# Front of a hybrid attention kernel by batch, with gate keys over all 102 rows

## The reference

```python
x = x + attn_a(layernorm(x), W)
x = x + ffn(layernorm(x), gate_w, expert_bias, w1, w2, w3)
x = x + attn_b(layernorm(x), ...)
x = x + ffn(layernorm(x), ...)

def attn_a(x, W):                    # B, T, C = 4, 512, 128; 16 heads of 8
    q, k, v, gate = split(x @ W.T)   # 128, 128, 128, 16 columns
    log_G = cumsum(log_sigmoid(gate), axis=time)
    S = Q @ K.T                      # a head
    Z = 2*log(abs(S) + 1e-7) + log(scale) + log_G[t] - log_G[s]
    Z = where(s <= t, Z, -inf)
    P = exp(Z - rowmax(Z))
    return (P @ V) / sum(P)
```

## Time and profile before

| | before |
|---|---|
| median of the timed runs | 573.21 us |
| span of the profiled execution | 602.3 us |
| PE busy | 470.7 us (78%) |
| DVE busy | 334.1 us (55%) |
| ACT busy | 334.9 us (56%) |
| POOL busy | 305.8 us (51%) |
| mean granted TensorE clock | 0.857 |

### The profile page before, as it was taken

How to read it: one execution, slowest core, us unless ns; L and a number is a source line. 1 busy time by engine, 2 the same in 40 slices (tenths; PEclk the granted TensorE clock), 3 DMA queues, 4 the chain that set the end, 5 groups by cost and what they waited for, 6 DMA issues and landing times. The chain is left out here.

```text
span 602.3 us, 11488 instructions
## 1 busy us (share of the span) xinstructions
PE 470.7 (78%) x3813; PEld 332.8 (55%) x3813; DVE 334.1 (55%) x786; ACT 334.9 (56%) x656; POOL 305.8 (51%) x323
## 2 busy tenths in 40 slices
PE   2745998889989688789885897994789876779891
PEld 1333575556556455457564575773457664457670
DVE  4747884875885898232561276746366737032121
ACT  1553895876796766635652355465356445334350
POOL 3102573564473326837637475743565842566651
PEclk9985695977798676899998799998799988798896
DMA  5065064153165910201311311112311112241213
GB/s 143 6 142 99 7 156 83 42 120 69 23 151 174 196 74 10 56 23 43 73 65 47 95 41 40 29 35 87 110 35 32 38 30 87 59 125 42 47 37 118
DMA packets 36563, 43.52 MB, mean 72 GB/s; under 512 B 5996, under 2 KB 31492, under 8 KB 36484
## 3 DMA queue, kind: packets, MB, share of 16 engines
q1 hardware_dynamic: 30620, 30.72, 20.1%
q0 software_dynamic: 5888, 12.07, 8.1%
HBM read 25.91 MB, written 15.86 MB: 69 GB/s over the span
## 5 line engine op out<-in xcount | busy, mean ns | idle before, releaser
L1295 POOL DMA_INDIRECT token_out<-ysb,id_out x92 | 93.6, 1017 | 112.0 <-ACT ysb L1454 88.1
L933 POOL TENSOR_TENSOR PP<-PP,E 128x512 f32<-128x512 f32 x64 | 82.3, 1287 | 96.3 <-ACT PP L884 96.1
L1514 DVE TENSOR_TENSOR hid<-silu,ps 128x352 f32<-128x352 f32 x92 | 47.8, 520 | 147.1 <-PE ps L1376 87.9
L837 DVE TENSOR_SCALAR A<-ps 128x1024 int32<-128x1024 int32 x80 | 96.7, 1221 | 29.0 <-PE ps L742 26.5
L1287 POOL DMA_INDIRECT tiled<-scaled_rows,id_in x92 | 91.5, 995 | 26.7 <-issue 24.0
L884 ACT ACTIVATE PP<-A,feps 128x1024 f32<-128x1024 f32 x80 | 91.9, 1149 | 15.9 <-DVE A L837 15.8
L1355 ACT ACTIVATE turned<-ps 128x512 f32<-128x512 f32 (+2 forms) x104 | 56.9, 547 | 73.1 <-PE ps L1343 49.7
L1389 PE MATMUL ps<-room,turned 128*128 x552 | 82.0, 287 | 18.1 <-ACT ysb L1454 15.6
L1373 PE MATMUL ps<-room,turned 128*128 x184 | 78.7, 511 | 17.8 <-ACT silu L1447 14.0
L1389 PEld LDWEIGHTS ps<-room,turned 128*128 128x128 f32 x552 | 72.5, 200 | 21.7 <-issue 21.6
L1376 PE MATMUL ps<-room,turned 128*128 x184 | 75.6, 495 | 0.0
(11 more groups left out here) (211 smaller groups left out, 651.7 us busy)
## 6 DMA issues: line engine op xcount, KB each, us to landing
QS<-parts SPq DMA_DIRECT2D x24, 192.0 KB
KS<-parts SPq DMA_DIRECT2D x24, 192.0 KB
parts<-room SPq DMA_DIRECT2D x32, 128.0 KB, 2.4
scaled_rows<-xT SPq DMA_DIRECT2D x8, 512.0 KB
yb<-token_out SPq DMA_DIRECT2D x8, 512.0 KB, 4.0
room<-in_L_ffn_w_dram SPq DMA_DIRECT2D x2, 1408.0 KB, 9.2
tiled<-scaled_rows,id_in POOLq DMA_INDIRECT x92
token_out<-ysb,id_out POOLq DMA_INDIRECT x92
```

The source lines that it names most:

```text
L837: v.tensor_scalar(A[:, U % 3, :].bitcast(I32), ps[:, bank:bank + 2, :].rearrange("p k t -> p (k t)").bitcast(I32), 0x7fffffff, None, ALU.b ...
L933: g.tensor_tensor(w, w, E[:, hh % 4, :], MUL).then_inc(s_PD, 1)
L1295: g.indirect_dma_start(yr_d[m], bass.IndirectOffsetOnAxis(ap=id_out[:, m % 2, s:s + 1], axis=0), ysb[:, J % OUTS, :], None).then_inc(s_ret ...
L1514: v.tensor_tensor(hid[:, J % 2, 0:HID], silu[:, J % 2, :], ps[:, BK_B + J % 2, 0:HID], MUL).then_inc(s_hid, 1)
```

## The change

- Norms go by batch, each batch waits for its own part of x; the weights are loaded behind the first batch's x.
- K is projected ahead of Q. The gates' inputs are copied ahead of the values.
- The gates go in two units, batch 0 and batches 1 to 3; the bounds in three, 0, 1, and 2 with 3. The maximum over partitions is a turn on TensorE, a maximum of the row on DVE, a diagonal of it, and a product with ones, in place of POOL's reduction.
- Batch 0 and 1's parts are made by DVE alone in the front. The first stack is read for four heads first, K's rows ahead of Q's.
- The totals, parts, rows and differences of the second gate unit, the last bound and the clears stand in slots 0 to 8 (`FRONT`). Up to slot 9 the differences use one bank.
- The keys of the gates hold 102 rows, zeros in 0 to 95, set by POOL once; the products of the differences run over all 102 rows of QS.

```diff
-        def gate_keys(G, r):
-            own, n = slice(96, 102), T // 2
-            free = xh[own, (2 + G % 2) * TB:(3 + G % 2) * TB, :].rearrange("p i c -> p (i c)")
...
-            return (free[:, 0:n], free[:, n:2 * n], *other)[r].bitcast(BF16)
+        def gate_keys(G, r, own=slice(0, 102)):
+            n = T // 2
+            if G % 2 == 0:
+                return tiled[own, 4 * C + n * r:4 * C + n * r + n].bitcast(BF16)
+            free = xh[own, 3 * TB:4 * TB, :].rearrange("p i c -> p (i c)")
+            return (free[:, 0:n], free[:, n:2 * n], WT[own, 0:n], keys[own, :])[r].bitcast(BF16)
+
+        def key_rows_pool(odd):
+
+            g = nc.gpsimd
+            if not odd:
+                g.wait_ge(s_std, B)
+                link(g.memset(tiled[0:96, 4 * C:12 * C], 0.0), who="pool")
+                g.memset(tiled[96:99, 4 * C:12 * C].bitcast(BF16), 1.0).then_inc(s_ones, 1)
+                g.wait_ge(s_ones, 1)
+                return
+            g.wait_ge(s_const, NCONST)
+            g.wait_ge(s_vzp, B)
+            for r in range(GH):
+                link(g.memset(gate_keys(1, r, slice(0, 96)).bitcast(F32), 0.0), who="pool")
+                ones3 = g.memset(gate_keys(1, r, slice(96, 99)), 1.0)
+                if r < GH - 1:
+                    link(ones3, who="pool")
+            ones3.then_inc(s_ones, 1)
+            g.wait_ge(s_ones, 2)
...
+        GATE_UNITS = ((0,), (1, 2, 3))
+        BOUND_UNITS = ((0,), (1,), (2, 3))
+        BK_M = 7
...
             for b in range(B):
-                sp.dma_start(xt[:, TB * b:TB * b + TB, :], x_rows[:, TB * b:TB * b + TB, :]).then_inc(s_x, 16)
-            sp.dma_start(Wrows[:, :, :], W[0:3 * C, :].rearrange("(n p) c -> p n c", p=P)).then_inc(s_w, 16)
-            sp.dma_start(Wgr[:, :], W[3 * C:3 * C + H, :]).then_inc(s_w, 16)
-            sp.dma_start(gwr[:, :], gate_w).then_inc(s_w, 16)
+                sp.dma_start(xt[:, TB * b:TB * b + TB, :], x_rows[:, TB * b:TB * b + TB, :]).then_inc(s_x[b], 16)
+                if b == 0:
+                    sp.dma_start(Wrows[:, :, :], W[0:3 * C, :].rearrange("(n p) c -> p n c", p=P)).then_inc(s_w, 16)
+                    sp.dma_start(Wgr[:, :], W[3 * C:3 * C + H, :]).then_inc(s_w, 16)
+                    sp.dma_start(gwr[:, :], gate_w).then_inc(s_w, 16)
...
             sp, b = nc.sync, G // NG
             if G < 2:
-                sp.wait_ge(s_vzp, 3 + G)
-                for r in range(GH):
-                    gates = gate_keys(G, r)[0:3].rearrange("p (n c) -> p n c", c=P)
-                    sp.dma_start(gates, bc(onesb[0:3, :].unsqueeze(1), [3, gates.shape[1], P])).then_inc(s_keys[G], 16)
+                sp.wait_ge(s_ones, G + 1)
             else:
                 sp.wait_ge(s_D, GH * (G - 1))
             for r in range(GH):
-                sp.dma_start(gate_keys(G, r)[3:6], gates_d[b, 1, :, GH * (G % NG) + r, :]).then_inc(s_keys[G % 2], 16)
+                sp.dma_start(gate_keys(G, r, slice(99, 102)), gates_d[b, 1, :, GH * (G % NG) + r, :]).then_inc(s_keys[G % 2], 16)
...
+        def first_stack_sync():
+
+            sp = nc.sync
+            sp.wait_ge(s_part, 4)
+            store_sync(0, 1)
+            sp.wait_ge(s_store, 16 * 5)
+            rows_of_sync(0, 0, 1, 0, GH, s_early)
+            sp.wait_ge(s_part, PARTS)
+            store_sync(0, 0)
+            sp.wait_ge(s_store, STORES)
+            rows_of_sync(0, 0, 0, 0, GH, s_early)
+            gates_sync(0)
+            sp.dma_start(QS[96:99, 0, 0:8, :], gates_d[0, 0, :, 0:8, :]).then_inc(s_early, 16)
+            keys_sync(0)
+            rows_of_sync(0, 0, 1, GH, GH, s_stack[0])
+            rows_of_sync(0, 0, 0, GH, GH, s_stack[0])
+            keys_sync(1)
...
+            rows_of_sync(b, slot, 0, 8 * half, 8, s_stack[slot])
+            rows_of_sync(b, slot, 1, 8 * half, 8, s_stack[slot])
...
-            norm_root_half(1)
-            bound_pool(0)
+            for b in range(1, B):
+                norm_root(0, b)
+            key_rows_pool(False)
...
-            bound_pool(1)
+            key_rows_pool(True)
...
+        def bound_turn_tensor(u):
+            pe = nc.tensor
+            bs = BOUND_UNITS[u]
+            n = 2 * len(bs)
+            pe.wait_ge(s_mx, 2 * (bs[-1] + 1))
+            if u == 0:
+                pe.wait_ge(s_wTc, 2)
+            pe.transpose(ps[0:n, BK_M, 0:P], mx[:, bs[0]:bs[-1] + 1, :].rearrange("p b n -> p (b n)"), ident[:, :]).then_inc(s_mxt, 1)
+
+        def bound_spread_tensor(u):
+            pe = nc.tensor
+            n = 2 * len(BOUND_UNITS[u])
+            pe.wait_ge(s_most, u + 1)
+            pe.matmul(ps[:, BK_M, P:P + n], ones[0:n, :], mostd[0:n, u, 0:n], start=True, stop=True).then_inc(s_mxa, 1)
...
+        def gate_sums_tensor(u):
 
             pe = nc.tensor
-            pe.wait_ge(s_lg, hf + 1)
+            pe.wait_ge(s_lg, u + 1)
             pe.wait_ge(s_const, 5)
-            if hf:
+            if u:
                 pe.wait_ge(s_gt, 1)
-            for o, m in ((0, tri), (HT * H, ones)):
-                ins = pe.matmul(ps[:, 6, o:o + HT * H], m[:, :], lg[:, HT * hf:HT * hf + HT, :].rearrange("p t h -> p (t h)"),
+            t, n = unit_tiles(u), TB * H * len(GATE_UNITS[u])
+            for o, m in ((0, tri), (n, ones)):
+                ins = pe.matmul(ps[:, 6, o:o + n], m[:, :], lg[:, t, :].rearrange("p t h -> p (t h)"), start=True, stop=True)
+            ins.then_inc(s_gp, 1)
...
+            src = ps[:, 4:6, :].rearrange("p k (n c) -> p (k n) c", n=2)
+            a.activation(z[:, batch(b), :], src[:, :, C:C + H], ACT.Copy).then_inc(s_z, 1)
...
+            for k in range(2):
+                i = TB * b + 2 * k
+                src = ps[:, 4 + k, :].rearrange("p (n c) -> p n c", n=2)[:, :, 0:C]
+                ins = a.activation(va[:, i:i + 2, :, 0:HS], src.rearrange("p n (h d) -> p n h d", h=H), ACT.Copy)
+            ins.then_inc(s_vz, 1)
+
...
         AT_NORMAL = (8, 9, 10)
+        FRONT = {'totals': 0, 'parts': 1, 'rows': {2: 1, 3: 2, 4: 3}, 'differences': 5, 'clear': {1: 5, 3: 6},
+                 'bounds': {5: 2, 6: 3}, 'most': 7, 'scale': 8}
+        T_STARTS = 10
...
-                other = len(diff_banks) % 2 and U not in X_TAKEN and U < X_ENDS
+                other = len(diff_banks) % 2 and U not in X_TAKEN and T_STARTS <= U < X_ENDS
...
-            if p == 0 and half == 0:
-                pe.wait_ge(s_stack[slot], STACKS * (b + 1))
+            if p == 0 and G == 0:
+                pe.wait_ge(s_early, 16 * 7)
+            elif p == 0 and (half == 0 or G == 1):
+                pe.wait_ge(s_stack[slot], stacked(n))
             if p == 0:
-                pe.wait_ge(s_keys[G % 2], 16 * GH * (G // 2 + 2))
+                if G < 2:
+                    pe.wait_ge(s_ones, G + 1)
+                pe.wait_ge(s_keys[G % 2], 16 * GH * (G // 2 + 1))
...
-                    pe.matmul(dst[:, P * j:P * j + P], gate_keys(G, r)[:, P * j:P * j + P], QS[96:102, slot, h, P * j:P * j + P],
+                    pe.matmul(dst[:, P * j:P * j + P], gate_keys(G, r)[:, P * j:P * j + P], QS[:, slot, h, P * j:P * j + P],
...
+                if U == FRONT['totals']:
+                    gate_sums_tensor(1)
+                if U in FRONT['rows']:
+                    gate_turn_tensor(FRONT['rows'][U])
+                if U == FRONT['most']:
+                    bound_turn_tensor(2)
+                if U == FRONT['scale']:
+                    bound_spread_tensor(2)
...
-            v.wait_ge(s_vz, 2 * B)
-            for k in (BK_OFF, BK_DIA):
-                v.memset(ps[:, k, :], 0.0).then_inc(s_zb, 1)
...
-                if b + 1 < B and k in (0, 3, 4, 7, 8):
+                if U == FRONT['totals']:
+                    gate_totals_vector(1)
+                if U == FRONT['parts']:
+                    gate_parts_vector(1)
+                if U in FRONT['rows']:
+                    gate_rows_vector(FRONT['rows'][U])
+                if U == FRONT['differences']:
+                    gate_differences_vector(1)
+                if U in FRONT['bounds']:
+                    for n in range(2):
+                        bound_vector(FRONT['bounds'][U], n)
+                if U == FRONT['most']:
+                    bound_most_vector(2)
+                if U == FRONT['scale']:
+                    bound_scale_vector(2)
+                if U in FRONT['clear']:
+                    if U == 1:
+                        v.wait_ge(s_vz, B)
+                    v.memset(ps[:, FRONT['clear'][U], :], 0.0).then_inc(s_zb, 1)
+                if 0 < b < B - 1 and k in (0, 3, 4, 7, 8):
                     parts_vector(b + 1, k)
...
+            if p == 0 and G % NG == 0:
+                a.wait_ge(s_fs, bound_unit(G // NG) + 1)
...
+                if U == FRONT['differences'] + 1:
+                    decays_scalar(1)
+                if 0 < b < B - 1 and k in (1, 2, 5, 6):
                     parts_scalar(b + 1, k)
...
+            first_stack_sync()
```

(78 more changed lines are left out.)

263 lines of the change are left out of this document (141 added, 122 removed).

## The result

The changed kernel takes 554.94 us (median of 5 runs, 554.23 to 560.08), the kernel before in the same sitting 573.86 (5 runs, 571.23 to 578.62): ratio 0.9721, 95% interval 0.9676 to 0.9766. By the ratio that is 16 us less (13 to 19). The two medians lie further apart, 18.9 us; I go by the ratios on record throughout. The forecast was 10.5 us less, a ratio of 0.982, with 549 to 573 as its range. The direction and most steps were right; the gain was put 5 us too small.

The account below looks back on a forecast made before the run. Bound by a front chain over all four batches, then slots paced by PE (low clock) or ACT (high clock). 6.5 + 4 + 0.5 = 11 us, scaled by 0.952 to 10.5, gives 562.7 us; range 549 to 573.

Parts of the forecast that it names:

- The front: From start to first score product: a chain over all four batches; by batch, A(0) at about 45, 9.5 us earlier.
- The detour over TensorE: Front, bound's maximum: two small TensorE products and two DVE steps replace POOL's reduction; 1.3 us taken, between 0.9 and 4.
- The costliest step: Front, PE: gate sums of batch 0 ahead of batch 1's projection, PE standing from about 17 to 24.
- The first slots: Slots 0 to 8: 12.1 us of moved work makes DVE the bound, 23.4 us for nine; A(10) at 69.7.
- rival D: Slots 0 to 8: DVE's in-order waits for PE, 1.5 us at each of six stages, make it slower: 578; chance 0.11.
- Slots 10 to 19: Lighter than before, 1.65 us each at the high clock by ACT's pace; A(20) at 87 by the stack's chain.
- 102 rows: Differences over 102 rows: gaps around 6-row products go, paying only where PE is the bound; 4 us taken of 5.5.
- The clock: Low stretch from 92 to 106 may stay at 1.00 if PE's stall goes: up to 4 us, 0.5 taken.
- The scale: Sum times 0.952, timed median 573.2 over profiled span 602.3: 11 us becomes 10.5.
- C: Rival, given back: the stack's chain and DVE's nine slots leave A(20) within 2 us of before: 571 to 573; chance 0.12.
- B: Rival: the products keep their bubbles or ACT takes the pace, so only 6 us gained: 567; chance 0.20.
- A: Rival, much more: PE bounds nearly everywhere after slot 10 and the clock stays up, 23 us gained: 550; chance 0.15.

Follow-up runs that it names:

- bounds by POOL: Changed kernel with the three maxima over partitions by POOL's reduction again, in place of turn, diagonal and product: 566.38 us, ratio 0.9911.
- all in front: Changed kernel with the second gate unit, last bound and clears done ahead of slot 0 instead of in slots 0 to 8: 564.92 us, ratio 0.9903.
- projection first: Changed kernel with PE taking batch 1's projection ahead of batch 0's gate sums: 553.49 us, ratio 0.9701; a second time 552.05 us, 0.9633.
- spread early: Changed kernel with batch 1's projection ahead of the gate sums, plus the last bound's product ahead of slot 8's 48 sum products: 553.22 us, ratio 0.9668.
- before again: The kernel before, without an edit, timed and traced a second time: 570.6 us, ratio 0.9985.
- six rows: Changed kernel with the differences over the 6 gate rows again, all else as changed: 561.43 us, ratio 0.9832.
- 102 rows only: Kernel before with only the gate keys and differences over 102 rows, zeros set by POOL: 565.21 us, ratio 0.9879.

## Why the prediction was right, and where its size was off

**The front.** Right nearly step by step: transfers at 3.6 (forecast 4.0), the maximum at 15.6 (15.0), PE standing from 17.7 to 24.6 (17 to 24), the log of batch 0 at 24.3 (23.7), the turn of batch 1's bound at 39.0 (40), the last log at 44.7 (44.5), A(0) at 45.0 (about 45). The detour over TensorE took from 15.57 to 17.76, 2.2 us, where I took 1.3 between 0.9 and 4; 0.9 of it is PE still in batch 0's projection and the turn of batch 1. One sentence was wrong: the last log didn't wait for ACT in the same way, it stood behind the Q parts in DVE's queue. What I never priced is POOL's side: the 6.84 us of idle time ahead of the IOTA stood in the trace before, and with it the reductions' price. By "bounds by POOL" it is 10 us to go back on the products, by "all in front" 10 to go back on the slots: each alone undoes all that the front gives (9.6), so these prices don't add up, the edits need each other. The sum didn't suffer, since it was built forward from the new chain and not as a difference, but it couldn't have said which edit earns the gain.

**The costliest step.** Gate sums ahead of projection 1 cost 2.6 to 4 us at A(0), as "projection first" shows, but only 1 to 3 in the time. "Costs most of what is won" overstated it.

**The first slots.** Nine took 24.1 us, 2.68 each (2.6), A(10) is at 70.3 (69.7). DVE was not full, though: of the 3.4 us of idle time in 23, 2.25 were the wait of rival D, one stage of six; at the others it was 0.6 or less, below the 1 us from which D decides. And "spread early" shows that even this one cost nothing.

**Slots 10 to 19.** ACT's pace as forecast, but from one A to the next 1.55 us and not 1.65. ACT casts no parts in slots 10 to 19 of either kernel; it is the rows: in before again and six rows it is 1.65 as well, in 102 rows only 1.55. And the stall at slot 20 is gone, where I left 1 us. A(20) is at 85.8 (87): 7.3 us earlier than in the second execution of before, 6.5 forecast.

**102 rows.** This is a term of the sum that was mis-sized: 4 us taken, 6.4 to 6.9 measured, though the intervals (from 3) don't exclude 4. The step that failed is "Where ACT or DVE is the bound it costs and gives nothing": at the high clock, with ACT as the bound, five slots went from 8.19 to 7.96 us. The steps were right (0.86 and 0.42 against 0.85 and 0.43; 0.45 and 0.23 against 0.43 and 0.22): both gaps went. That they would go with the 6 rows was my expectation, since the earlier trace rows shows the gaps alone; the runs showed it, for six rows, with the order and the banks of the changed kernel, has both again (medians of 247 and 242 ns at the low clock, where the changed kernel has 107 and 107; 152 and 147 at the high one, where it has 56 and 56). Why a gap stands there no run shows. I took 5.5 at the pace of PE, cut it to 4, and had no term for a higher clock with them.

**The clock.** Its term, 0.5, rested on the stretch at 0.52 behind the standing PE in one execution. The second execution had 1.7 us of standing and 1.00 from 92 to 106, so that reading doesn't hold; the low stretch belonged to that one execution. The rest of the change gave 9.6 us (7 to 12) where the front and the clock together had 6.7, so about half of the shortfall is here. By the traces six rows is 6.7 us ahead of before again at A(20), as forecast, and gains 3.7 more up to A(79), at 0.81 against 0.79; which edit brings that stays open.

**The scale.** The sum was multiplied by 0.952 because one long profile stood against shorter timed runs. The second execution spans 568.3 against 570.6 timed, so the factor had no ground: all but 3 of the 34 us of excess lay behind the attention, in stages that the change doesn't touch. It took only 0.5 us off.

**Rivals.** C and B fall: nothing was given back behind slot 10, and the rows gave 6. A's mechanism holds in part, the clock (0.77 and 0.79 to 0.85 and 0.87) and 6 of its 14 us of rows, without its size: ACT is the bound of the slots at the high clock (20.00 of 20.00 us busy from 72 to 92). D falls: one wait of 2.2 us instead of six of 1.5.

## What to carry to other kernels

Look at what stands ahead of an operation on its engine before calling it cheap: a reduction over partitions on POOL was 0.4 us of work and 12 us of hand-over (5.6 ahead of it and 6.8 behind), lost within the interval where nobody waited for it (0.9745 against 0.9721) and 10 us for three whose results DVE waited for. Work that the first unit doesn't need belongs into the slots behind it, even when these then run at that engine's pace: 16 us of it cost 9 there. Products on 6 rows between products on 102 and 128 rows cost a gap at either change, 0.14 us at 1.2 GHz and 0.1 at 2.4 (102 and 128 rows beside each other don't: steps of 107 and 56 ns in the changed kernel); filling the unused rows with zeros takes the gap away, and no run here shows a cost of it. An engine that is busy nearly all the time can still be waiting once a group for another (8.19 us a group against 7.96 here): read the step of a whole group, not the busy share. And look at a second execution before building on the clock of one stretch.

## What the runs showed of the hardware that I had not expected

- POOL: 5.5 to 5.9 us ahead of a reduction over partitions, and 6.8 to 7.6 us of idle time ahead of the next IOTA or TENSOR_TENSOR behind one, with a record of a change of its configuration at the start of each; memsets and affine selects between run at once (22.36 and 22.70 behind the reduction of 22.11 in "bounds by POOL").
- TensorE: between products on 102 rows and on 6 rows 0.14 us at 1.2 GHz and 0.1 at 2.4 GHz (a step of 247 ns against 107 at the low clock and 152 against 56 at the high, from the last score product to the first of 6 rows; 242 and 147 from the last of 6 rows to the mask; medians over the 64 heads of the kernel before).
- The granted clock from A(20) to A(79) was 0.77, 0.79 and 0.81 in the three traces with such gaps and 0.85 to 0.88 in the ten without them. That the gaps are the cause is likely, not shown.
